# Projecting the values of two pairs of heads at a time in a fused attention kernel

## The reference

```python
x = layernorm(x + L0_attn(x))   # causal attention, 16 heads of 64
x = layernorm(x + L0_ffn(x))    # gated attention, 8 heads
x = layernorm(x + L1_attn(x))   # attention, 16 heads of 64, position bias
x = layernorm(x + L1_ffn(x))    # top-k experts
```

## Time and profile before

| | |
|---|---|
| median of 3 runs | 5007.32 us (5004.74 to 5010.79) |
| profiled execution | 5006.9 us, span of the profile 5005.3 us |
| TensorE matmul (PE) busy | 4148.6 us, 83% of the span |
| VectorE (DVE) | 3618.9 us, 72% |
| GpSimd (POOL) | 3000.5 us, 60% |
| ScalarE (ACT) | 1977.1 us, 39% |
| pairs of the first attention | from 80 to 1240 us |
| pairs of the second 16-head attention | from 3103 to about 4775 us |

### The profile page before, as it was taken

How to read it: one execution, slowest core, us unless ns; L and a number is a source line. 1 busy time by engine, 2 the same in 40 slices (tenths; PEclk the granted TensorE clock), 3 DMA queues, 4 the chain that set the end, 5 groups by cost and what they waited for, 6 DMA issues and landing times. The chain is left out here.

```text
span 5005.3 us, 63352 instructions
## 1 busy us (share of the span) xinstructions
PE 4148.6 (83%) x22330; PEld 2152.8 (43%) x22330; DVE 3618.9 (72%) x5957; ACT 1977.1 (39%) x3403; POOL 3000.5 (60%) x2548
## 2 busy tenths in 40 slices
PE   6999999999388788778778755999999999999947
PEld 3454545445154344344444322444444444444416
DVE  4877778777287777767777743888788788878835
ACT  2443434434154345345334321444344344434410
POOL 2665656556166787678778761666566566656720
PEclk9999999999689899989899965999999999999976
DMA  0000000000410000000000004121121121221020
GB/s 27 1 1 9 1 1 9 1 5 1 129 40 24 16 24 24 25 16 24 29 16 17 5 21 60 26 39 26 26 47 26 26 47 26 35 34 26 17 60 17
DMA packets 98044, 125.91 MB, mean 25 GB/s; under 512 B 28896, under 2 KB 76448, under 8 KB 97728
## 3 DMA queue, kind: packets, MB, share of 16 engines
q1 hardware_dynamic: 97728, 121.86, 11.2%
HBM read 103.69 MB, written 18.12 MB: 24 GB/s over the span
## 5 line engine op out<-in xcount | busy, mean ns | idle before, releaser
L767 POOL TENSOR_TENSOR s_psum_p<-s_psum_p,s_prob 128x1024 f32<-128x1024 f32 (+3 forms) x640 | 1352.3, 2113 | 417.9 <-ACT s_prob L521 379.1
L521 ACT ACTIVATE s_prob<-s_sT 128x1024 f32<-128x1024 f32 (+2 forms) x896 | 836.4, 933 | 970.0 <-DVE s_sT L651 476.4
L429 PE MATMUL s_pv<-s_prob,s_vp 128*64 128x512 f32 (+3 forms) x3584 | 889.3, 575 | 3.4 <-POOL s_prob L752 2.5
L767 POOL TENSOR_TENSOR s_psum_p<-s_prob 128x1024 f32<-128x1024 f32 (+1 forms) x128 | 286.9, 2241 | 603.3 <-ACT s_prob L521 600.7
L656 DVE RECIPROCAL s_recip<-s_recip 128x128 f32<-128x128 f32 x512 | 481.5, 942 | 98.5 <-ACT s_recip L471 98.5
L1677 POOL TENSOR_TENSOR s_psum_p<-s_psum_p,s_prob 128x1024 f32<-128x1024 f32 x192 | 461.8, 2405 | 136.7 <-ACT s_prob L1398 135.1
L385 PE MATMUL s_mx<-s_bh,s_ah 64*128 64x512 f32 (+3 forms) x1792 | 389.8, 431 | 183.2 <-DVE s_bm L592 84.1
L602 DVE CUSTOM_DVE_ANT_0 s_mx<-s_mx,s_strip 128x512 f32<-128x512 f32 x640 | 429.6, 713 | 111.7 <-PE s_mx L385 110.8
L404 PE MATMUL s_sT<-s_ah,s_bh 64*128 64x512 f32 (+3 forms) x1792 | 414.7, 459 | 19.1 <-ACT s_prob L521 18.9
L592 DVE TENSOR_REDUCE s_bm<-s_mx 128x8 f32<-128x1024 f32 (+3 forms) x384 | 362.5, 944 | 51.6 <-PE s_mx L385 42.8
L1398 ACT ACTIVATE s_prob<-s_sT 128x1024 f32<-128x1024 f32 x256 | 264.9, 1035 | 304.0 <-PE s_sT L1251 300.4
(11 more groups left out here) (238 smaller groups left out, 8457.2 us busy)
## 6 DMA issues: line engine op xcount, KB each, us to landing
s_strip<-bias_rows SPq DMA_DIRECT2D x256, 144.0 KB, 5.8
s_wr<-gated_weights SPq DMA_DIRECT2D x32, 960.0 KB, 4.8
s_near<-bias_rows SPq DMA_DIRECT2D x256, 48.0 KB, 2.0
x<-s_x SPq DMA_DIRECT2D x12, 512.0 KB, 2.9
s_x<-x SPq DMA_DIRECT2D x8, 512.0 KB, 5.1
s_x<-in_L_attn_x_dram SPq DMA_DIRECT2D x4, 512.0 KB, 4.0
m_xtok<-x SPq DMA_DIRECT2D x4, 512.0 KB, 5.6
out_dram<-m_xnew SPq DMA_DIRECT2D x4, 512.0 KB, 3.2
```

What stands on the lines that cost most here:

```text
L429: last = mm(pv[heads(hd), lo:CH], vp[:, g % 2, j, heads(hd)], prob[:, k % PR, hd, lo:CH], start=j == 0, stop=end)
L521: nc.scalar.activation(prob[:, k % PR, :, lo:CH], sT[:, k % 2, :, lo:CH], ACT.Exp, scale=st.scale).then_inc(exp_done, 1)
L767: nc.gpsimd.tensor_tensor(out[:, :, lo:CH], src, p[:, :, lo:CH], ALU.add)\
```

## The change

Two pairs' values are projected together. A job now takes two blocks of tokens and the weight columns of two pairs, with 6 matmuls of 256 columns. Four jobs make the values of two pairs, all in the odd pair before them, and even pairs have none. ScalarE copies each job with two instructions of 256 columns, one for each pair's slot of `vp`, which gets a third slot. The order of the three products within a block changes as well. The jobs before pair 0 go from two to four.

```diff
-        value = lambda u, k: out[u].append(("v", g + 1, k)) if g + 1 < GP else None
+        value = lambda u, k: out[u].append(("v", (g + 1) // 2, k)) if g % 2 and g + 1 < GP else None
...
             if turn:
-                plan = {"v": (3, 4), "xt": (5, 7), "item": (8, 9, 10, 11)}
+                plan = {"v": (), "xt": (5, 7), "item": (8, 9, 10, 11)}
             elif after:
-                plan = {"item": (0, 1, 3, 4), "v": (5, 7), "y": (8, 9), "t": (10, 11)}
+                plan = {"item": (0, 1, 3, 4), "v": (), "y": (8, 9), "t": (10, 11)}
             else:
-                plan = {"item": (0, 1, 3, 4), "v": (8, 10)}
+                plan = {"item": (0, 1, 3, 4), "v": (5, 7, 8, 10)}
         else:
             if turn:
-                plan = {"v": (3, 5), "xt": (7, 8), "item": (9, 11, 13, 15)}
+                plan = {"v": (), "xt": (7, 8), "item": (9, 11, 13, 15)}
             elif after:
-                plan = {"item": (0, 1, 3, 4), "v": (5, 6), "y": (8, 9), "t": (11, 12)}
+                plan = {"item": (0, 1, 3, 4), "v": (), "y": (8, 9), "t": (11, 12)}
             else:
-                plan = {"item": (0, 3, 5, 7), "v": (8, 12)}
+                plan = {"item": (0, 3, 5, 7), "v": (1, 8, 11, 13)}
...
-        vp = sb("vp", [P, 2, NB, P])
+        vp = sb("vp", [P, 3, NB, P])
...
                 elif kind == "v":
-                    cols = slice((of % NPAIR) * P, (of % NPAIR + 1) * P)
-                    for n in range(4):
-                        o, rows = misc[:, n * P:(n + 1) * P], slice((4 * k + n) * P, (4 * k + n + 1) * P)
+                    p = 2 * of % NPAIR
+                    cols = slice(p * P, (p + 2) * P)
+                    for n in range(2):
+                        o, rows = misc[:, 2 * n * P:2 * (n + 1) * P], slice((2 * k + n) * P, (2 * k + n + 1) * P)
                         mm(o, xh[:, rows], wv[:, 0, cols], start=True, stop=False)
-                        mm(o, xl[:, rows], wv[:, 0, cols], start=False, stop=False)
-                        last = mm(o, xh[:, rows], wv[:, 1, cols], start=False, stop=True)
+                        mm(o, xh[:, rows], wv[:, 1, cols], start=False, stop=False)
+                        last = mm(o, xl[:, rows], wv[:, 0, cols], start=False, stop=True)
                     last.then_inc(v_full, 1)
...
                 elif kind == "v":
-                    act.wait_ge(v_full, 2 * of + k + 1)
-                    if of >= 2:
-                        act.wait_ge(pv_done, (of - 1) * U)
-                    copy(vp[:, of % 2, 4 * k:4 * k + 4, :].rearrange("p i n -> p (i n)"), misc[:, :])\
-                        .then_inc(v_done, 1)
+                    act.wait_ge(v_full, 4 * of + k + 1)
+                    if of >= 1:
+                        act.wait_ge(pv_done, (2 * of - 1) * U)
+                    both = misc[:, :].rearrange("p (i a n) -> p i a n", i=2, a=2)
+                    for a in range(2):
+                        copy(vp[:, (2 * of + a) % 3, 2 * k:2 * k + 2, :], both[:, :, a, :]).then_inc(v_done, 1)
```

More of the change, by code:

```diff
@@ L311, in misc_free @@
                 elif kind == "v":
-                    pe.wait_ge(v_done, 2 * of + k + 1)
+                    pe.wait_ge(v_done, 2 * (4 * of + k + 1))
                 elif kind == "rs":
@@ L421, in values @@
                     if c == 0:
-                        pe.wait_ge(v_done, 2 * g + 2)
+                        pe.wait_ge(v_done, 8 * (g // 2 + 1))
                 if st.causal and j >= 4 * c:
@@ L428, in values @@
                 for hd in range(2):
-                    last = mm(pv[heads(hd), lo:CH], vp[:, g % 2, j, heads(hd)], prob[:, k % PR, hd, lo:CH],
+                    last = mm(pv[heads(hd), lo:CH], vp[:, g % 3, j, heads(hd)], prob[:, k % PR, hd, lo:CH],
                               start=j == 0, stop=end)
@@ L437, in _ @@
                 misc_job(("item", 0, k))
-            for k in range(2):
+            for k in range(4):
                 misc_job(("v", 0, k))
```

## The result

The kernel after the change took 4998.3 us, the median of 20 runs (4987.4 to 5008.3); the kernel before took 5005.2 beside it, also 20 runs (4996.6 to 5013.5). The ratio is 0.9983, with a 95% interval of 0.9977 to 0.9989. That is a gain of 0.17%, some 7 us by the medians and 8.5 by the ratio, where I had forecast 30. It lies just outside my range (4948 to 4997), in the case I had called *No difference*.

The account below looks back on a forecast made before the run. TensorE's work, busy over 92%, was taken to set most of the time, with VectorE close behind. Causal -24.1, biased -12.1, set-up +3.8 and clock +2 gave -30.4 from 5006.9, so 4976 us; range 4948 to 4997.

Parts of the forecast that it names:

- No difference: Whole kernel: clock falls in new waits, or stretched VectorE instructions, give back the gain; from 4993 us on, chance 0.14.
- Clock: Falls to 1.2 GHz, a few more at the new wait in unit 9 of even causal pairs: +2 us.
- rival 3: New waits in even pairs bring clock falls, or GpSimd additions stretch VectorE instructions: 30 us back, 5007; chance 0.14.
- Even ordinary, causal: Ten causal pairs losing two jobs: the first wins 0, the second 1.39 us; -14 us in all.
- Turn: Three causal pairs losing the jobs in units 3 and 4: -2.27 us each, -6.8 in all.
- After: Three causal pairs losing two jobs and the 0.65 us wait in unit 5: -3.6 us each, -10.8 in all.
- Odd, causal: Fifteen causal pairs with four new jobs for two old: +0.5 us each, +7.5 in all.
- The causal sum: All pair kinds of the causal attention together: -14 - 6.8 - 10.8 + 7.5 = -24.1 us.
- Biased: Biased attention: even ordinary -7.3 us, turn and after pairs -14.4, odd pairs +9.6; together -12.1.
- Set-up: Jobs before pair 0, which nothing covers, go from two to four: +1.9 us per attention, +3.8 in all.
- Rival 1: Whole kernel: TensorE's work is the time, so all 78 us come back but for the set-up: 4933; chance 0.10.
- Rival 4: New jobs: a 256-column matmul costs what a 512-column one does, 0.23 us, making the kernel slower, 5057; chance 0.08.

Follow-up runs that it names:

- warm_after: Changed kernel plus fillers (repeated score matmuls, nothing new computed) in TensorE's waits in causal units 3 and 9 and biased unit 14: 4956.33 us, 0.9911.
- warm_before: Kernel before the change plus fillers (repeated score matmuls) in unit 3 of every causal pair alone: 4987.97 us, 0.9974.
- warm_moved: Changed kernel with fillers in old and new waits, odd biased pairs' jobs moved from units 1, 8, 11, 13 to 6, 8, 12, 13: 4942.54 us, 0.9879.

## Why the prediction was wrong

The mechanism of the work was right. The step that failed is the one under **Clock**: "The wait of about 1.4 us that now opens in unit 9 of even causal pairs may bring a few more. I add +2." It is a term that was put far too small. In the profiled executions it was 6 more falls in the causal attention and 5 more in the biased one, 11 x 1.5 = 16 us. By the medians it is more: the change's work was worth 28.6 us between the two kernels next to free of falls, and 7 to 8.5 were left in the 20 runs, so the falls took 20 to 22 us where my sum has 2. Their price of 1.5 us each comes out of `warm_after` as well: its profiled execution is 36.4 us and 25 falls (pair 0's with them) under the changed kernel's. The remaining 4 us between 28.6 and the forecast 32.4 are errors in the terms below. That is the first half of rival 3 ("20 falls at 1.5 us"), to which I gave 0.14. I argued against it with the mean clock of 1.00 in the biased attention, but that was the clock of a kernel without the wait of 1.90 us in it. I also looked only at the wait that the change opens in unit 9. Of the falls that came anew, 6 stand behind the old wait in unit 3, where TensorE's next matmuls are unchanged, 6 at the biased attention's new wait, and only 3 behind the one that I had named; 4 of before are gone.

Term by term, without falls (pairs of `warm_before` and `warm_after`, from the first scores of a pair to those of the next):

- **Even ordinary, causal**: 34.9 to 33.6 us, -1.35 each (forecast -1.39). Three of them (pairs 10, 18 and 26) gave only -0.7, since their unit 0 grew by 0.6, to about 3.5. In unit 0 of pair 10 the last product of the scores waits for VectorE (its L675 in the kernels with fillers, the maxima's rows), and VectorE comes late from the layer norm of the sequence before, whose multiplication took 2.46 us. All ten: -12, forecast -14.
- **Turn**: 37.5 to 35.1, three times, -7 (forecast -6.8).
- **After**: 50.3 to 48.2 in pair 24, the only one that no fall in either touches, -2.1 each and -6 in all, where I had -10.8. Two waits gave back what I had left out. In unit 6 TensorE now waits 0.57 us for the maxima, as I had reckoned for the odd pairs but not here; the unit is 0.86 longer. And I wrote that the long output projection "gives nothing back". It does, 0.69 us: it now waits for VectorE's normalization, which was covered before. The waits of TensorE in the causal attention, after the change (us in total, times, longest):

```profile
PE s_mx L386 <- DVE s_bm L594: 80.0, 95, 1.6
PE s_misc L351 <- DVE s_bl L570: 10.0, 15, 0.7
...
PE s_misc L366 <- DVE s_z L664: 2.0, 3, 0.7
```

  The last row is new, 0.7 us in each of the three after pairs. The second is the wait before the job of unit 5, 15 times, as forecast. The first was 72.3 us before.
- **Odd, causal**: 34.9 to 35.1, +0.2 (forecast +0.5). Units 5 and 6 together changed by +0.78 (forecast +0.94), unit 7 by +0.90 (+0.87), units 8 and 10 by -1.17 (-1.22). VectorE's slack before the maxima of unit 9 gave back 0.32, where I had allowed 0.1.
- **The causal sum**: pairs 0 to 30 took 1142.4 us in `warm_before` and 1116.0 in `warm_after`; less two falls at 1.5 that is -23.4, against -24.1 forecast. It is close by luck: the after pairs gave 4.5 us less than forecast, and the odd pairs cost 4.5 less.
- **Biased**: even ordinary 50.9 to 50.1 (forecast -0.73), but the last pair but one gave 0 (46.8 both), since TensorE meets the same waits there in units 8 and 14. Turn and after pairs -2.05 and -2.4 (forecast -2.4). Odd +0.75 (forecast +0.64): units 1 and 2 together changed by +0.7 (forecast +0.85), unit 8 by -0.6, unit 11 by +0.9, since the half that was to be hidden was not, and units 12 to 14 by -0.26 (forecast 0). In all 1634.7 to 1625.6, -9.1 against -12.1.
- **Set-up**: the first scores start 1.6 us later in the profiled pair of kernels and 2.85 later in the pair with fillers; the second attention's, +0.2 and +0.6. I had 1.9 for each. (I read the lower clock there from the matmuls of 128 columns, 0.21 us apart instead of 0.11; the trace before has no record of the clock ahead of 85 us, and the one after shows 0.50 in the same stretch.) Nothing behind the biased attention changed by more than 1.1.

In the profile after itself this reads: the causal pairs -14.6, which is -23.4 and six falls; the biased pairs 1636.5 to 1634.7, -1.8, which is -9.1 and five falls; +1.6 and +0.2 for the set-ups. The sum, -14.6, is the difference of the spans, 5005.3 and 4990.7. That pair of profiles is kinder than the medians by 7 us: it shows the mechanism, the 20 runs the size.

Rival 1 (TensorE's work is the time, 4933) falls with the waits of 1.61 and 1.90 us. Rival 4 (the price of 256 columns) falls with the pitch of 0.12. The other half of rival 3, stretched VectorE instructions, did not occur: 2.33 and 2.21 us as before. The Trainium skill's page "SBUF — State Buffer", section "Who interferes with whom", says that a VectorE instruction with two inputs in SBUF contends with a GpSimd instruction that reads it. The trace agrees: in pair 10 GpSimd's addition ran from 476.71 to 479.09 us and the normalization ended 0.55 us behind it, as before the change.

What stays open is why the old wait brings a fall in some pairs and none in others of the same kind, and how units far ahead of it bear on that.

## What to carry to other kernels

Where TensorE's work is removed in front of a wait on another engine, the saving turns into idle time, and idle time of 1.4 to 1.9 us can cost clock for the matmuls behind it. Falls can also become more frequent at places the change never touched. So price the falls of the clock as a term of their own: count them in the trace before, note which waits they stand behind, old and new, and measure against a version with both kernels' waits filled. If such waits can't be closed with useful work, repeating a matmul in them is worth trying; here that made a gain of 0.2% one of 0.9%, and with the jobs placed in idle time 1.2%.

## What was not expected of the hardware

- Adding TensorE work made the kernel faster. Four pairs of matmuls in each of the 32 causal pairs, 32 x 0.93 = 30 us of work, took 27 us off the changed kernel (0.9983 to 0.9930), and 13 off the kernel before by the ratio (0.9974), 15.5 by the medians.
- A mean clock of 0.97 or 1.00 over an attention hides this. The falls have to be counted: each is 3.4 us at 0.50, and takes 1.5 us.
- The waits before a fall need not be long: the three of the after pairs before the change stood behind 0.39 and 0.65 us. And the wait of 1.39 us had none behind it in half of the pairs after the change and in two thirds of them before.
- The falls come pair after pair at the same place (from 834.3 and from 868.5; from 1097.2, 1134.7 and 1168.8), and then stay away for some pairs.
- The spread of the runs goes with them: 21 us over the 20 runs after the change and 17 over the 20 before; 7 us over the 11 of `warm_before`, 2 over the four of `warm_after`, 4 over the four of `warm_moved`.
